# State-space scan: partitions of a tile ordered channel by channel instead of state by state

## What is computed

```python
x = x + attn_a(layernorm(x))     # 16 heads of 8, mask: sliding window of 32 or every 64th row
x = x + ffn(layernorm(x))        # three layers of +1/-1 weights, relu between
x = x + attn_b(layernorm(x))     # a selective state-space block
x = x + ffn(layernorm(x))        # the same weights again
```

```python
dt = softplus(dt_lo @ W_dt + b_dt)                 # (batch, time, 256)
A  = -exp(A_log)                                   # (256, 16)
h[e, n] = exp(dt[e] * A[e, n]) * h[e, n] + dt[e] * u[e] * B[n]      # over time
y[e]    = sum over n of h[e, n] * C[n]
```

## Time and profile before

| what | us |
|---|---|
| median of 3 runs | 1010.6 (1006.17 to 1012.24) |
| the profiled execution, its own time | 1010.07 |
| its span, first to last instruction | 1008.3 |
| busy in the span: PE, DVE, ACT, POOL | 777.3, 690.9, 646.0, 609.3 |
| granted TensorE clock, mean | 0.885 of full |

### The profile page before, as it was taken

How to read it: one execution, slowest core, us unless ns; L and a number is a source line. 1 busy time by engine, 2 the same in 40 slices (tenths; PEclk the granted TensorE clock), 3 DMA queues, 4 the chain that set the end, 5 groups by cost and what they waited for, 6 DMA issues and landing times. The chain is left out here.

```text
span 1008.3 us, 21855 instructions
## 1 busy us (share of the span) xinstructions
PE 777.3 (77%) x8036; PEld 433.7 (43%) x8036; DVE 690.9 (69%) x1138; ACT 646.0 (64%) x1282; POOL 609.3 (60%) x598
## 2 busy tenths in 40 slices
PE   7889889795959689795879868686948595848678
PEld 5665436343534265363543443343514341223336
DVE  7974468585948669682867777677768493747583
ACT  5786768694949669674668766576647353625343
POOL 4032457585739666682875576685759573947391
PEclk9999979897979979897889979697969798888779
DMA  4000122123121221222022222222222222222310
GB/s 163 4 3 2 58 110 109 74 95 118 61 102 43 108 93 74 88 77 102 34 105 87 102 110 93 106 84 101 93 85 77 107 73 102 77 102 88 117 69 22
DMA packets 41931, 83.60 MB, mean 83 GB/s; under 512 B 2009, under 2 KB 2658, under 8 KB 41826
## 3 DMA queue, kind: packets, MB, share of 16 engines
q1 hardware_dynamic: 41826, 82.22, 21.9%
HBM read 71.20 MB, written 11.01 MB: 82 GB/s over the span
## 5 line engine op out<-in xcount | busy, mean ns | idle before, releaser
L1803 POOL TENSOR_TENSOR d<-d,cr 128x1024 f32<-128x1024 f32 x128 | 299.7, 2350 | 46.4 <-issue 14.6
L1621 ACT ACTIVATE ps<-dt,An 128x512 f32<-128x512 f32 x252 | 172.2, 693 | 207.3 <-DMA dt<-dtd 137.5
L1292 DVE TENSOR_TENSOR d<-ps,du 128x512 f32<-128x512 f32 x173 | 114.2, 679 | 142.9 <-DMA du<-dud 72.6
L1304 DVE TENSOR_TENSOR_SCAN d<-ps,d 128x512 f32<-128x512 f32 x128 | 151.4, 1210 | 47.1 <-ACT ps L1621 42.9
L1304 DVE TENSOR_TENSOR_SCAN d<-ps,hl,d 128x512 f32<-128x512 f32 x128 | 158.3, 1267 | 26.1 <-ACT ps L1621 23.9
L1789 POOL TENSOR_TENSOR d<-du,br 128x512 f32<-128x512 f32 x79 | 99.7, 1271 | 106.0 <-DMA du<-dud 31.6
L885 PE MATMUL ps<-h,w 128*128 128x512 f16 (+1 forms) x512 | 123.8, 397 | 27.7 <-DVE h L1236 15.0
L885 PEld LDWEIGHTS ps<-h,w 128*128 128x128 f16 x512 | 49.5, 102 | 105.2 <-DVE h L1236 27.9
L974 PE MATMUL ps<-d,cst 128*32 128x512 f32 x512 | 75.5, 666 | 19.7 <-POOL d L1803 19.6
L823 PE MATMUL ps<-cst,sx 128*128 128x128 f32 x384 | 60.0, 297 | 27.2 <-ACT sx L1452 15.4
L896 PE MATMUL ps<-w,h 128*128 128x128 f32 x496 | 63.8, 285 | 12.7 <-ACT h L1518 12.7
(11 more groups left out here) (185 smaller groups left out, 1448.1 us busy)
## 6 DMA issues: line engine op xcount, KB each, us to landing
cr<-bcd SPq DMA_DIRECT2D x64, 256.0 KB
br<-bcd SPq DMA_DIRECT2D x64, 256.0 KB
dt<-dtd SPq DMA_DIRECT2D x64, 256.0 KB
du<-dud SPq DMA_DIRECT2D x64, 256.0 KB
dtd<-sR SPq DMA_DIRECT2D x16, 256.0 KB, 5.5
dud<-sE SPq DMA_DIRECT2D x16, 256.0 KB
X<-in_x SPq DMA_DIRECT2D x8, 256.0 KB, 6.0
out<-X SPq DMA_DIRECT2D x3, 512.0 KB, 12.5
```

Source lines behind the costliest of these rows:

```text
L1292: eng.tensor_tensor(d, PB[:, :], DU[:, q, :], ALU.mult).then_inc(v_dr, 1)
L1304: eng.tensor_tensor_scan(d, banks[u % NG][:, :], d, hl[:, r:r + 1] if m % 2 else 0.0, ALU.mult, ALU.add).then_inc(v_sc, 1)
L1621: eng.activation(banks[u % NG][:, :], src[:, :], ACT.Exp, scale=An[:, g:g + 1]).then_inc(s_da, 1)
L1803: eng.tensor_tensor(d, d, CR[k % NC][:, :].unsqueeze(1).to_broadcast((128, n, 512)), ALU.mult).then_inc(p_cm, n)
```

## The change

The partitions of a tile change places: partition p now holds channel p // 4 and state p % 4. The two source views are transposed to (32, 4, 512): for B and C the 32 copies are outermost and the four rows inner, for dt and dt * u the 32 rows are outermost and the four copies inner. The summing weights become a table of their own, `csel` (128 x 32), with ones where p // 4 is the channel; `spread` gets ones where the row's channel is p // 4; the packed A_log is transposed to match. The table of constants grows by 32 columns, so that the first load of weights has 339.5 KB where it had 323.5 KB. No instruction is added or taken away on any engine, and the order of all queues, the buffers and the waits stay.

```diff
-for _name, _n in (("ident", 128), ("qmask", 4), ("one8", 1), ("rmask", 2), ("spread", 128)):
+for _name, _n in (("ident", 128), ("qmask", 4), ("csel", 32), ("one8", 1), ("rmask", 2), ("spread", 128)):
...
-    put("spread", (p[:, None] % 32 == p[None, :] % 32).astype(np.float32))
+    put("csel", (p[:, None] // 4 == np.arange(32)[None, :]).astype(np.float32))
+    put("spread", (p[:, None] % 32 == p[None, :] // 4).astype(np.float32))
...
             def states(k, at):
 
                 at += 4 * (k % 4)
-                return bcd[k // 8 % 2][at:at + 4, :].unsqueeze(1).to_broadcast((4, 32, 512))
+                return bcd[k // 8 % 2][at:at + 4, :].unsqueeze(0).to_broadcast((32, 4, 512))
...
             def rows(src, n, q):
 
                 e = 128 * (n % 2) + 32 * q
-                return src[n // 2 % 2][e:e + 32, :].unsqueeze(0).to_broadcast((4, 32, 512))
+                return src[n // 2 % 2][e:e + 32, :].unsqueeze(1).to_broadcast((32, 4, 512))
...
-                    t = eng.matmul(bank[32 * q:32 * q + 32, :], spread[:, 0:32], D[:, (4 * k + q) % ND, :],
+                    t = eng.matmul(bank[32 * q:32 * q + 32, :], csel, D[:, (4 * k + q) % ND, :],
                                    start=(w == 0), stop=(w == 3))
...
-    al = a["attn_b_A_log"].reshape(2, 4, 32, 4, 4).transpose(4, 2, 0, 3, 1).reshape(128, 32)
+    al = a["attn_b_A_log"].reshape(2, 4, 32, 4, 4).transpose(2, 4, 0, 3, 1).reshape(128, 32)
```

More of the change, by code:

```diff
@@ L471, in const @@
             return cst[0:rows, at:at + n]
-        ident, qmask, one8, rmask, spread = (const(n) for n in ("ident", "qmask", "one8", "rmask", "spread"))
+        ident, qmask, csel, one8, rmask, spread = (const(n) for n in ("ident", "qmask", "csel", "one8", "rmask", "spread"))
         masks = sb("masks", [128, 288], BF16)
```

## The result

| | before | after |
|---|---|---|
| median, us | 1008.71 (4 runs, 1006.17 to 1012.24) | 778.96 (4 runs, 777.77 to 779.42) |
| profiled execution, own time; span | 1010.07; 1008.3 | 779.12; 777.3 |
| granted clock, mean of the span | 0.885 | 0.989 |

The ratio is 0.7719 with a 95% interval from 0.769 to 0.7747. The forecast was 855 us with a range of 790 to 930. The time fell on the forecast side, but by 230 us where 155 were forecast, and 11 us past the low end of the range. The nearest case was the rival "more overlap goes than I count" (789 us, chance 0.11). Lines of the kernel after are one higher than before.

The account below looks back on a forecast made before the run. Replicated tiles waiting in line on a path of four of sixteen DMA engines were taken as the bound. 1010.07 less ACT's 154.7 us of such waits, all else at nothing, gave 855 us; range 790 to 930.

Parts of the forecast that it names:

- more overlap goes than I count: Rival: DVE's and POOL's waits are partly apart from ACT's and the clock returns in full; 789 us, chance 0.11.
- What bounds the kernel: Tile-scanning stage, 100 to 980 us: engines wait 318.0 us for replicated tiles queued on a four-engine DMA path.
- The source views: Replicating DMAs: 32 outermost instead of 4 gives 16 engines, 0.65 us a transfer instead of 2.4 to 2.57.
- Hot rows: Rival: for br and cr all engines read the same four rows, so part of the line stays; 900 us, chance 0.05.
- nothing changes: Rival: the engine count hangs on something other than outermost size, share stays 0.26; 1010 us, chance 0.03.
- slower: Rival: br and cr transfers become longer than 2.4 us on all 16 engines; 1119 us at 5 us each, chance 0.03.
- What the waits are worth: DMA waits of ACT, DVE and POOL in the scan stage: 154.7 of 318.0 us come back, giving 855.4 us.
- The check from PE's side: Scan stage from PE's busy time at 15% idle: 916 us at clock 0.87, 850 us at 0.95.
- The rest: csel, the packed A_log, the larger first weight load and SBUF places moved by 128 bytes: counted at nothing.
- The range: Whole kernel, 8 in 10: 790 to 930 us, taking in the forecast and the first three rivals in the main.

Follow-up runs that it names:

- dt alone: The changed kernel with only dt on the transposed source view, while dt * u, B and C keep the old one: 912.76 us.
- dt * u alone: The changed kernel with only dt * u on the transposed source view, the other streams on the old one: 905.73 us.

## Why the prediction was right and wrong

*What bounds the kernel* was right: a path of four DMA engines, with SP and all other DMAs in a line behind it. The share of 0.26, the packet counts with 2, 8 and 16 engines and the times with 2 and 8 show it. But that this path is "nearly always in use" was misread. The 0.24 of the stage also counts the stores and the other DMAs; by the prediction's own prices of 2.4 to 2.57 us the 256 transfers fill 614 to 658 of the 880 us, 70 to 75%. The line forms in bursts: SP's 64 issues of br took 0.52 us in the median and 4.39 us at most.

*The source views* were right. 32 outermost gives 16 engines. The Trainium skill's rule ("DMA: Bandwidth & Descriptors", section "Why a DMA increments its semaphore by 16 and not by 1") gives 16, 8 and 2 for outermost sizes of 32 or 16, 8 and 2 against 128 partitions. The packet counts agree with each. Landings of 3.2 to 3.7 us are above my "2 to 3 us" and within the 2 to 4 us named later.

*Hot rows* was no term. B and C, for which all engines read the same four rows, land in 3.2 and 3.3 us, faster than dt and dt * u with 3.6 and 3.7. The rivals *nothing changes* and *slower* fell with the share.

*What the waits are worth* is the step that failed. It said: the longest engine's 154.7 us, since the tile late to ACT "is usually late for DVE or POOL too", and "what DVE and POOL wait beyond it I set against new waits". Both halves were wrong. Of the 163 us beyond the 154.7, only 58 lie on another engine's wait; the other 105 us are apart in time. dt alone brought 94 us, dt * u alone 101, both 192. And few new waits came to set against them: 260 us had at least one engine in such a wait, and 231 us of span went. The scan's and the decay's waits for each other did not grow but fell, from 136.0 to 47.9 us; most of them had passed on late tiles. The term was put at 154.7 of 318.0 us, a factor of 0.49; it measured 231, a factor of 0.73.

Each engine here has one order. A us that ACT lost for dt moved its later decays, and the scan's queue behind them; a us that DVE lost later for dt * u came on top of it. This reading fits ACT's idle time, which fell by 225 us where its own waits for DMAs were 154.7. I had asked whether the waits fall on the same tile, where it counts whether they fall on the same moment.

*The check from PE's side* agreed with 855 by luck. It took over PE's idle share of the first 100 us (15%). The stage after has 7% (603.97 of 649). It also took a clock of 0.95; it was 0.99. With 7% and 0.99 the same sum gives 668.20 x 0.87 / 0.99 / 0.93 = 631 us, near the 649. The idle share of the first 100 us, where POOL is busy 28% of the time, was no measure for the stage. And the 64 us of PE's busy time that went as the clock rose are no cause of the gain: in the kernel before, a lower clock cost nothing. What raised the clock was not tried by itself; PE's stalls went in the same step.

*The rest* (csel, the constants, 128 bytes) was right at nothing: 778.21 us against 778.96.

*The range*: its low end was the rival of 789, "more overlap goes than I count". That rival had the right mechanism, but its price came from a guess of PE's idle share (10%) and not from the waits. An end from the sum of all entries (1010 - 318 = 692) was in the text as a bound and was left out of the range on the strength of the argument that failed.

## What to carry to other kernels

Waits of different engines in a pipeline of ordered queues add up unless they lie at the same moment. To price them, lay the waits over each other on the time axis and take the time in which at least one engine waits: here 260 us, of which 231 came back. The sum of the entries and the largest engine's share are only the two ends, and the lower end is not the likeliest. What a busy engine's slower clock costs, and what matmuls that compute nothing are worth, must be asked again once another bound is gone.

## What was not expected of the hardware

With 16 engines the transfers themselves take longer in the records: 33.1% of 16 engines over 777.3 us against 21.9% over 1008.3 us, which is 1.17 times the engine time for the same bytes. With eight engines it is 1.05 times (28.9% over 799.1 us). The two burst stretches above move 199 and 326 GB/s, not the 406 of the loads at the start. What slows them was not tried. The kernel hardly waits for it: 3.2 us of waits for these DMAs are left.
